# A two-layer recurrence on one core: the first layer's chain issued first, the second layer behind U, and (z - 1) h computed from z alone

## What is computed

```
# layer 1, a gated unit with hidden state h (32 x 256)
z  = sigmoid(x_t Wz + h Uz + vz)
r  = sigmoid(x_t Wr + h Ur + vr)
hh = tanh(x_t W + (r*h) U + vh)
h  = (1 - z)*h + z*hh            ; x1_t = x_t + h
# layer 2, a leaky cell with hidden state h1 (32 x 256)
g  = sigmoid(h1 Wh^T + x1_t Wz1^T + b)
h1 = tanh(h1*(1 - alpha) + g*x1_t) ; x2_t = x1_t + h1
```

## Time and profile before

| what | value |
|---|---|
| median of 3 runs | 1011.36 us (1010.21 to 1012.88) |
| span of the profiled execution | 1009.4 us |
| PE busy | 958.2 us (95%) |
| PEld busy | 794.0 us (79%) |
| DVE busy | 824.3 us (82%) |
| ACT busy | 619.9 us (61%) |
| POOL busy | 185.6 us (18%) |

### The profile page before, as it was taken

How to read it: one execution, slowest core, us unless ns; L and a number is a source line. 1 busy time by engine, 2 the same in 40 slices (tenths; PEclk the granted TensorE clock), 3 DMA queues, 4 the chain that set the end, 5 groups by cost and what they waited for, 6 DMA issues and landing times.

```text
span 1009.4 us, 112576 instructions
## 1 busy us (share of the span) xinstructions
PE 958.2 (95%) x50964; PEld 794.0 (79%) x50964; DVE 824.3 (82%) x2500; ACT 619.9 (61%) x2798; POOL 185.6 (18%) x390
## 2 busy tenths in 40 slices
PE   5699999999999999999999998699999999999987
PEld 4699999999999999999999994255666666556655
DVE  2377787777877778877787774999999999999993
ACT  2578777777777877877777773334444544344430
POOL 0011111111111111111111111223322222222220
PEclk7899999999999999999999999889999999999999
DMA  6122331300101001010010101001000000011001
GB/s 214 48 85 73 106 102 43 117 26 23 36 26 34 26 23 36 26 34 26 23 36 23 36 26 36 6 1 40 31 23 23 23 23 23 23 33 37 23 23 42
DMA packets 38295, 42.02 MB, mean 42 GB/s; under 512 B 5120, under 2 KB 31232, under 8 KB 37120
## 3 DMA queue, kind: packets, MB, share of 16 engines
q1 hardware_dynamic: 36832, 40.55, 12.8%
q10 hardware_dynamic: 1440, 1.18, 0.4%
HBM read 32.80 MB, written 8.91 MB: 41 GB/s over the span
## 4 chain that ended last, share of the span: by engine, by line
PE 54%; DVE 32%; issue 7%; ACT 4%; DMA 1%; DVEq 1%; ACTq 1%; POOL 0%; POOLq 0%
PE bank L755 30%; PE bank L702 21%; DVE arena L618 10%; DVE wx L630 4%; DVE cx L634 4%; ACT cand_kept L368 2%; DVE cx L643 2%; DVE cx L647 2%; DVE wx L616 2%; DVE cx L639 2%; DVE none_h L555 2%; DVE y L658 2%; DMA bias<-in_bias 1%; PE bank L873 1%; PE bank L844 1%
## 5 line engine op out<-in xcount | busy, mean ns | idle before, releaser
L702 PE MATMUL bank<-x_ahead,wx 128*32 128x64 f32 x12376 | 344.0, 223 | 7.8 <-issue 4.6
L702 PEld LDWEIGHTS bank<-x_ahead,wx 128*32 128x32 f32 x12376 | 238.5, 110 | 8.2 <-issue 8.2
L755 PE MATMUL bank<-none_h,urz 128*32 128x32 f32 x16384 | 205.2, 199 | 4.1 <-issue 0.8
L755 PEld LDWEIGHTS bank<-none_h,urz 128*32 128x32 f32 x16384 | 182.6, 110 | 19.6 <-DVE none_h L555 13.1
L266 POOL TENSOR_TENSOR x<-x_f,h_gx 128x64 f32 x256 | 88.7, 346 | 534.1 <-PE bank L755 533.0
L873 PE MATMUL bank<-x,wl 128*128 (+1 forms) x384 | 179.4, 607 | 0.9 <-DVE rank_rows L597 0.9
L422 ACT ACTIVATE arena<-bank,bl 128x512 f32<-128x512 f32 x96 | 66.0, 687 | 159.6 <-PE bank L873 159.6
L755 PE MATMUL bank<-rh_f,uh 128*32 128x32 f32 x8192 | 150.8, 199 | 7.1 <-DVE rh_f L543 4.0
L873 PEld LDWEIGHTS bank<-x,wl 128*128 128x128 f32 x384 | 71.5, 192 | 81.1 <-issue 79.7
L755 PEld LDWEIGHTS bank<-rh_f,uh 128*32 128x32 f32 x8192 | 122.1, 111 | 9.1 <-DVE rh_f L543 7.0
L555 DVE TENSOR_TENSOR_SCAN none_h<-zero_z,cand_kept 128x64 f32<-128x64 f32 x512 | 121.5, 278 | 8.9 <-ACT cand_kept L368 7.4
(11 more groups left out here) (84 smaller groups left out, 1347.0 us busy)
## 6 DMA issues: line engine op xcount, KB each, us to landing
x_in<-in_x SPq DMA_DIRECT2D x34, 256.0 KB, 2.7
x_ahead<-in_x SPq DMA_DIRECT2D x130, 64.0 KB, 1.8
arena<-in_w SPq DMA_DIRECT2D x8, 1024.0 KB, 5.7
out<-y SPq DMA_DIRECT2D x32, 256.0 KB, 2.5
rank_rows<-in_bias_rows SPq DMA_DIRECT2D x1, 1024.0 KB, 4.8
arena<-scratch SPq DMA_DIRECT2D x64, 16.0 KB
cx<-in_cx SPq DMA_DIRECT2D x1, 768.0 KB, 4.4
wx<-in_wx SPq DMA_DIRECT2D x1, 768.0 KB, 6.7
```

The lines of the kernel that those rows point to most:

```text
L702: mm = pe.matmul(out[32 * j:32 * j + 32], weights(k, j, m), moving(k), start=False, stop=False, tile_position=(0, 32 * j), skip_group_chec ...
L755: mm = pe.matmul(out[32 * j:32 * j + 32], weights(k, j, m), moving(k), start=False, stop=k == 1, tile_position=(0, 32 * j), skip_group_che ...
```

## The change

Every engine's step is reordered. On PE the four fixed turns become one pattern: gates of layer 1, 4 quarters' worth of ahead products (two `ahead_first` pieces on even steps, `ahead_second` on odd ones), the candidate (U), then layer 2's gate, then the other 4 quarters of ahead products. No ahead product stands inside gates or candidate any more. Inside the gates both reset quarters of half 0 come first. On DVE, L575 and L581 of layer 2 move to the start of a step, ahead of `rh_f`; `x1_f` of the step before follows `rh_f`. On ACT, tanh of layer 2 moves behind the reset gates, its gate behind the candidate. Layer 2's state is now made one step later. `keep_f` and its ACT instruction are gone: DVE makes (z - 1) h from z with one `scalar_tensor_tensor`, the candidate is negated by tanh of the negated input, and the scan subtracts. POOL's `x2` waits for the update gate of layer 1 and not for layer 2's gate, and its last turn stands outside the loop. SP issues the second `x_in` of a turn later.

```diff
@@ SP @@
-                next_steps(n, 1)
+                    if c == 3 and not first:
+                        next_steps(n - 1, 1)
@@ POOL @@
-                    pool.wait_ge(gate_pre, s + LAG + 2)
+                    if last and u >= BODY - LAG - 1:
+                        pool.wait_ge(gate_pre, s + LAG + 2)
+                    else:
+                        pool.wait_ge(z_done, s + LAG + 2)
...
+            turn(TURNS - 1, last=True)
@@ ACT @@
                 act.activation(zero_z[:, u % 2, :, :, 1], pre_z[par][:, :, v, :], ACT.Sigmoid).then_inc(z_done, 1)
-                act.activation(keep_f[:], pre_z[par][:, :, v, :], ACT.Sigmoid, scale=-1.0).then_inc(z_done, 1)
...
-                                   ACT.Tanh).then_inc(cand_done, 1)
+                                   ACT.Tanh, scale=-1.0).then_inc(cand_done, 1)
...
-                    gates_first(n, u)
+                    reset_gate(n, u)
+                    if not first or u > LAG:
+                        second_state(n, u)
...
+                    update_gate(n, u)
+                    if u % STEPS == 0 and (u or not first):
...
+                        seed_gate(((u - STEPS) // STEPS) % 2)
+                    candidate(n, u)
+                    if not first or u >= LAG:
                         second_gate(n, u)
-                    candidate(n, u)
...
+                            act.wait_ge(gate_done, t - LAG + 1)
+                        seed_reset((u // STEPS) % 2, reset_seeded)
@@ DVE @@
-                dve.wait_ge(z_done, 2 * t + 2)
-                dve.tensor_tensor(cand_kept[:, u % 2, :, :, 1], keep_f[:], none_h[:, now, :, :, 1],
-                                  ALU.mult).then_inc(kept_done, 2)
+                dve.wait_ge(z_done, t + 1)
+                dve.scalar_tensor_tensor(cand_kept[:, u % 2, :, :, 1], zero_z[:, u % 2, :, :, 1], 1.0,
+                                         none_h[:, now, :, :, 1], ALU.subtract, ALU.mult).then_inc(kept_done, 1)
...
-                                           0.0, ALU.mult, ALU.add).then_inc(h_done, 1)
+                                           0.0, ALU.mult, ALU.subtract).then_inc(h_done, 1)
...
-                    reset_state(n, u)
-                    if second:
+                    if not first or u > LAG:
                         second_gated(n, u)
+                        second_sum(n, u)
+                    reset_state(u)
+                    if u:
+                        first_output(n, u - 1, first)
...
+                    kept_state(n, u)
                     next_state(n, u)
-                    if second:
-                        second_sum(n, u)
-                    first_output(n, u, first)
@@ PE, first_gates @@
                 reset(0, 0)
-                keep(0, 0)
-                keep(0, 1)
+                pe.wait_ge(cand_done, 2)
+                reset(0, 1)
+                update(0, 0)
                 pe.wait_ge(h_done, 2)
-                reset(1, 0, taken=h_done).then_inc(r_pre, 1)
-                reset(0, 1)
+                reset(1, 0, taken=(h_done, cand_done)).then_inc(r_pre, 1)
                 reset(1, 1).then_inc(r_pre, 1)
...
@@ PE, first_cand @@
                 cand(0, 0)
-                hole()
+                pe.wait_ge(r_done, 2)
+                cand(0, 1)
                 pe.wait_ge(rh_done, 2)
-                cand(1, 0).then_inc(cand_pre, 1)
-                cand(0, 1).then_inc(rh_done, -2)
+                cand(1, 0, taken=(rh_done, r_done)).then_inc(cand_pre, 1)
                 cand(1, 1).then_inc(cand_pre, 1)
...
@@ PE, turn @@
+                for u in range(LOOP):
+                    later = 1 - u // STEPS
+                    first_gates(u)
+                    if u % STEPS == 0:
+                        pe.wait_ge(ahead_loaded[later], 16)
+                        pe.wait_ge(reset_seeded, 2)
+                        ahead_first(later, 0, 0)
+                        ahead_first(later, 0, 1).then_inc(reset_seeded, -2)
+                    else:
+                        ahead_second((u - LAG) % LOOP, later)
+                    first_cand(u)
+                    second_gate(u)
+                    if u % STEPS == 0:
+                        ahead_first(later, 2, 0)
+                        ahead_first(later, 2, 1)
+                    else:
+                        ahead_first(later, 1, 0)
+                        ahead_first(later, 1, 1).then_inc(ahead_loaded[later], -16)
```

187 lines of the change are left out of this document (79 added, 108 removed).

## The result

The changed kernel takes 1022.96 us (median of 4 runs, 1022.33 to 1023.62) beside 1012.05 us for the kernel before on the same chip (4 runs, 1010.21 to 1012.88): ratio 1.0101, 95% interval 1.0087 to 1.0116. It is slower by 1%; 992 us and a gain were predicted, so both the side and the range were wrong.

What follows compares the result with a forecast made beforehand. Layer 1's chain, 2.22 us a step, was taken as the bound; at 2.12, four steps take 8.69 us against 9.04, 22.1 us less over 64 loops, minus 1.5 and 1 us elsewhere: 992 us, range 981 to 1008.

Steps and rivals of the forecast that it cites:

- The reading of the chain: Layer 1's chain from gates to next gates sets the step: 2.22 us before, 2.12 predicted after.
- rival 2: Layer 2's ring from `rh_f` to the next `rh_f` sets the step at 2.20 us, time 1007 us; chance 0.12.
- Rival 1: POOL's `x2` holds the scan at the shared port by 0.16 us, step 2.28, time 1022 us; chance 0.09.
- Rival 3: Reset gate comes no earlier, waiting for TensorE: 0.61 not 0.57, candidate 0.54, step 2.19, 1005 us; chance 0.09.
- The rest, 0.24 + 0.34, stays.: Layer 1's chain: tanh to scan 0.24 us and scan to next gates 0.34 us stay unchanged.
- TensorE: gates 0.58, then 32 wide loads 0.42: TensorE is free 1.00 us after the gates start, 0.03 before the candidate is wanted at 1.03.
- 1.99 us of own work: TensorE's loads per step: 1.15 us narrow plus 0.84 wide, from cadences of 0.0090 and 0.0131 us.
- 8.69: Four steps of TensorE's loop in us, 3 x 2.12 + 2.33, against 9.04 before.
- Loop ends: TensorE's loop end costs 0.32 us between two loads every fourth step, 0.21 of it bare, making that step 2.33.
- VectorE's loop end: Standing ahead of L586, it pushes L593 past its slack: 0.1 us for 15 turns, 1.5 us.
- GpSimd's exit: POOL leaves its loop a turn earlier, with a stall like TensorE's against one step of slack: 1 us.
- The upper end of the forecast's own range: 1002 us: gates to `r_f` 0.59, candidate 0.54, step 2.17, with 2 us more at the ends.

Runs made afterwards that it cites:

- e3: The changed kernel with POOL's `x2` released by layer 2's gate as before, not by the update gate: 1.0103 of before, 1024.1 us.
- e9: e1 with `keep_f` back (second sigmoid on ScalarE), the kept part made from it, candidate not negated, scan adding: 1.0018 of before, 1014.2 us.
- e1: The changed kernel with the wait for `cand_done` again ahead of the one for `kept_done` in `next_state`: 0.9994 of before, 1013.4 us.
- e2: The kernel before with the state scan's two waits exchanged, `kept_done` first and `cand_done` second: 1.0172 of before, 1030.4 us.
- e12: The changed kernel with only TensorE's wait for `x_ahead` moved up to the gates' sixth quarter: 1.0046 of before, 1017.8 us.
- e10: e1 with TensorE's wait for `x_ahead` moved up to the gates' sixth quarter, away from the `reset_seeded` wait: 0.9934 of before, 1005.5 us.
- e14: e10 with four matmuls fewer ahead of TensorE's unchanged loop, output not the reference's: 1.0111 of before, 1024.8 us.

## Why the prediction was wrong

**The reading of the chain held in the main.** With layer 2's tanh behind it the reset gate came 0.05 earlier (0.57 predicted, 0.59 measured), as it would if the tanh had held it; no run moved the tanh alone. Layer 2 fitted, and so rival 2 did not happen; VectorE waited for `r_f` in 44 of 229 steps and was just in time in the others. Rival 1's collision with GpSimd's port did not happen either (e3), and it has about the predicted size where it does, on the kept product (e9: 0.14 for 0.16). Rival 3's 0.61 was not reached; its candidate segment of 0.54 was met in even steps only once the double wait was gone (0.55; with it 0.59), and not in odd ones (0.52). The time of rival 1, 1022 us, was met by another mechanism, that is by chance.

**The step that failed first: "The rest, 0.24 + 0.34, stays."** The diff shows two wait lines swapped in `next_state`, and the order's row shows both names in the other order. I priced the arithmetic of the scan and not its waits. The 0.24 measured 0.30, e1 and e2 show that the order of the waits does it, and it cost 11 us.

**The second: "TensorE: gates 0.58, then 32 wide loads 0.42", and the 1.99 us of own work.** I took cadences of 0.0090 and 0.0131 us from single runs of loads. In after's rows 64 gate loads take 305.38 - 304.77 = 0.61, and the 64 narrow loads of candidate and layer 2's gate take 306.46 - 305.83 = 0.63, where both were put at 0.58. The wide ones were sized nearly right: the last of 32 starts at 305.38 + 0.52 - 0.11 = 305.79. The candidate's loads come at 1.06 and not at 1.03 because `rh_f` is at 0.59 + 0.23 = 0.82; they follow it by 0.24, as before. Own work is 2.11 and not 1.99. With 0.32 for a loop end this makes 4 x 2.11 + 0.32 = 8.76 us for four steps: the 8.69 that I predicted lay below what TensorE needs for itself.

**The third: the new order's double wait on TensorE had no term.** e12 and e10 price it at 0.09 and 0.14 for four steps.

**Loop ends** cost the 0.32 that was read, but the step was put at 2.33 and took 2.42 with its longer own work. VectorE's loop end (1.5 us) did not show in the medians of that step, and for GpSimd's exit (1 us) no wait shows. The upper end of the forecast's own range was added up a little low: 0.59 and 0.54 with 2 us more give 1003, not 1002, which changes nothing here.

**The sum.** Four steps: 9.27 measured, 8.69 predicted. The two waits are 0.29 of the 0.58. The other 0.29 is e10's 8.98 against 8.69, made of terms mis-sized by 0.01 to 0.04 each: gates to `r_f` 0.59 for 0.57, `r_f` to `rh_f` 0.23 for 0.21 (the pair of `r_f` takes 0.29 in after's rows and took 0.27 in the step that I read), the candidate 0.52 and in even steps 0.55 for 0.51, in three steps, and 0.09 in the fourth. Times 64 the loops are 37 us over; 2.5 us at the ends did not come, and about 4 us less passed between the last step's gates and the end (400.1 us before, 396.1 after), most of it the stall of 3.1. 37 - 2.5 - 4 = 30.5, and the span is 1020.5 - 989.8 = 30.7 over.

## What to carry to other kernels

Where an instruction waits for two semaphores, order them so that the instruction itself carries the one that comes last (here it carried the wait written first), and spread the others over earlier instructions of a full engine; read this off the order of the built program, since a diff hides it in two swapped lines. Size a full engine's work over whole steady steps, by step length less the idle time in it, and not by the cadence inside one run of loads. Before believing a difference of 1 or 2% between two versions of a looped TensorE kernel, look behind the loop's first loads for a hole that no wait explains, and shift the loop by a few matmuls, in the kernel before as well as in the one after.

## What the runs showed of the hardware

- Which of two waits became a separate instruction on VectorE moved tanh to scan by 0.06 to 0.07 us a step: 11 us in the new kernel, and about 12 of e2's 17 us in the old one; one separate wait of 0.05 us in a full TensorE stream cost 0.09 to 0.14 us per two even steps.
- TensorE's loop of 8 steps (3,072 matmul and weight-load instructions) was fetched in every iteration (421 packets of instructions), and the time nearly doubled (1.91 and 1.92) at a lower granted clock (0.76 and 0.68); one of 4 steps (1,536) was not (12 packets).
- With an unchanged loop, moving its start by four matmuls cost 18 us (1.0111 against 0.9934): with a hole of 0.228 us in each, the 64 loops are 64 x (9.19 - 8.98) = 13 us longer, the stall at the exit is 3.2, and the small rest stays open. The same program of before had holes of 0.06 us on average, and of 0.14 with two of VectorE's waits swapped (e2). The Trainium skill ("Runtime: NRT & Kernel Launch", Instruction fetch mechanics) says that a taken branch to a target outside the fetch window forces a transfer before execution goes on. e14's queue of instructions shows 12 packets, as e10's does, so no transfer stands behind this hole, and what else the fixed place is remains open.
